# Edge stages of a graph layer: sums stored three slots to a transfer, and loads issued by ScalarE

## The reference

```
h = (x @ W.T).reshape(n, H, D)
alpha = einsum(h[src], a_src) + einsum(h[dst], a_dst)
enc = relu(edge_attr @ edge_W.T + edge_b).reshape(-1, H, D)
alpha = alpha + sum(enc * h[dst], axis=-1)
alpha = where(alpha >= 0, alpha, 0.2 * alpha)
ex = exp(alpha - segment_max(alpha, dst)[dst])
attn = ex / max(segment_sum(ex, dst)[dst], 1e-10)
out = segment_sum(h[src] * attn[..., None], dst) + bias
```

## Time and profile before

| | us |
|---|---|
| median of 3 runs | 7718.56 |
| lowest and highest run | 7714.73 and 7724.49 |
| span of the profiled execution | 7807.0 |
| PE busy | 5257.7 (67%) |
| POOL busy | 3613.4 (46%) |
| DVE busy | 3278.9 (42%) |
| ACT busy | 1371.0 (18%) |

### The profile page before, as it was taken

The page is one execution under the profiler, slowest core; times in us unless marked ns, Lnnn a source line. Parts: engine busy times, 40 slices in busy tenths (PEclk is TensorE's granted clock), DMA queues, the critical chain, the costliest instruction groups (busy, mean ns, idle before and its releaser), DMA issues. The chain is left out here.

```text
span 7807.0 us, 99204 instructions
## 1 busy us (share of the span) xinstructions
PE 5257.7 (67%) x19729; PEld 3739.4 (48%) x19729; DVE 3278.9 (42%) x5938; ACT 1371.0 (18%) x2977; POOL 3613.4 (46%) x3708
## 2 busy tenths in 40 slices
PE   2387887788788878228999625556565556663498
PEld 1144444444444444227999514444444444442498
DVE  6255555555555555721111313333333333336244
ACT  2122222222222222002222200000000000000122
POOL 2635555555555554042222056666666666650222
PEclk9689999999999999658999857777777777786699
DMA  6434444444444443515666544444444444434255
GB/s 220 136 101 122 122 119 123 124 124 125 122 123 121 122 124 102 186 60 165 183 183 183 153 102 114 113 115 115 114 112 113 113 114 116 113 102 154 101 198 188
DMA packets 718013, 1022.24 MB, mean 131 GB/s; under 512 B 301733, under 2 KB 531561, under 8 KB 692608
## 3 DMA queue, kind: packets, MB, share of 16 engines
q0 software_dynamic: 183456, 485.95, 23.8%
q1 hardware_dynamic: 527676, 519.31, 21.7%
q10 hardware_dynamic: 6564, 14.14, 0.5%
HBM read 868.26 MB, written 153.27 MB: 131 GB/s over the span
## 5 line engine op out<-in xcount | busy, mean ns | idle before, releaser
L773 POOL DMA_INDIRECT e_rows<-sc_table,e_eidx x3224 | 3115.9, 966 | 2253.8 <-issue 952.6
L880 PE MATMUL e_ps_o<-e_rows,e_oh 128*128 128x264 f32 x6448 | 1918.5, 449 | 856.9 <-ACT e_res L969 700.8
L880 PEld LDWEIGHTS e_ps_o<-e_rows,e_oh 128*128 128x128 f32 x6448 | 1379.2, 222 | 1384.3 <-issue 1147.6
L1064 DVE SCALAR_TENSOR_TENSOR e_u<-e_encr,e_adst,e_ps_hd 128x512 f32<-128x512 f32 x806 | 597.1, 745 | 1160.2 <-remote 366.1
L1132 DVE TENSOR_TENSOR e_rows<-e_rows,e_ps_w 128x1024 f32<-128x1024 f32 x806 | 970.7, 1207 | 106.3 <-issue 83.5
L822 PE MATMUL e_ps_X<-e_u,e_hwide 128*104 128x512 f32 x1612 | 871.1, 635 | 16.8 <-DVE e_u L1064 14.8
L1055 DVE TENSOR_SCALAR e_ohT<-e_at,e_nid 96x512 bf16<-96x512 int16 x806 | 292.5, 363 | 1384.6 <-DMA e_aw<-sc_a2p 553.7
L969 ACT COPY e_res<-e_ps_o 32x264 f32<-32x264 f32 x806 | 296.0, 367 | 3291.4 <-PE e_ps_o L884 1242.4
L810 PE MATMUL e_ps_enc<-e_at,e_w_enc 96*128 96x512 bf16 x806 | 317.9, 394 | 570.6 <-ACT e_encr L942 383.4
L1676 PE MATMUL x_ps_h<-x_xT,x_w 128*128 128x256 f32 x2624 | 648.2, 405 | 15.4 <-DMA x_b<-in_L_ffn_b_dram 15.4
L1676 PEld LDWEIGHTS x_ps_h<-x_xT,x_w 128*128 128x128 f32 x2624 | 638.5, 337 | 20.6 <-issue 16.4
(11 more groups left out here) (290 smaller groups left out, 3538.7 us busy)
## 6 DMA issues: line engine op xcount, KB each, us to landing
x_w<-in_L_ffn_W_dram SPq DMA_DIRECT2D x112, 1024.0 KB
e_at<-sc_grp SPq DMA_DIRECT2D x403, 192.0 KB
x_w<-in_L_ffn_w_dram SPq DMA_DIRECT2D x60, 1024.0 KB
e_rows<-sc_table,e_eidx POOLq DMA_INDIRECT x3224
e_at<-sc_grp SPq DMA_DIRECT2D x403, 96.0 KB
sc_agg<-e_res SPq DMA_DIRECT2D x816, 33.0 KB
sc_xb<-r_zero SPq DMA_DIRECT2D x24, 1032.0 KB
x_xin<-sc_xb SPq DMA_DIRECT2D x86, 258.0 KB
```

Of the source, the lines that this page charges most:

```text
L773: pool.indirect_dma_start(rows[:, k, s, j, :], None, dr["table"][:, :], bass.IndirectOffsetOnAxis(eidx[:, k, s, j:j + 1], 0)).then_inc(s_r ...
L880: nc.tensor.matmul(ps_o[:, 0:ROW], oh[:, k, at_j:at_j + P], rows[:, k, s, j, :], start=(j == 0), stop=False)
L1064: nc.vector.scalar_tensor_tensor(u[:, p, h, :], encr[:, h, :], adst[:, h:h + 1], ps_hd[:, h, :], ALU.add, ALU.mult).then_inc(s_u, 1)
```

## The change

The sums are no longer stored at their window's first node. `agg` gets 20512 rows instead of 6272 and 32, and slot number t stores at rows 32 t and on. Five groups of slots per block (3, 3, 3, 3 and 1) are stored by one transfer each, at an address that needs no table. Five semaphores, one per group, tell when a group is stored, and `evict` waits for one of them at slots 0, 3, 6, 9 and 12 only.

SP issues the loads of the first 4 slots (layer 0) or 2 slots (layer 1). All others are issued by ACT, in the new `ahead`, at the end of its work for a slot: a `hold` on PE, a TENSOR_LOAD of two registers, and the two DMAs, for the slot 4 or 2 places further on. In the prologue, `ahead` follows the relus of each slot of block 0 and of block 1 (in layer 1 it stands there alone).

The r-stage has to find a node's sums. In the last two blocks of layer 0, DVE works out for each of the 49 tiles of 128 nodes the row of `agg` that holds it (49 passes over 128x640 numbers and about a dozen small ones), and the result is kept for both layers. The r-stage then fetches the sums by 49 indirect DMAs of POOL, 7 per chunk, instead of 7 plain loads (L1304). The planning stage clears more rows of `agg` (9 transfers instead of 8) and writes two small tables less.

```
 SP
-            def store(t, s, n):
-                hold(sp, s_out, t * 16 - (32 * SB - OUT0), s_ps)
-                hold(sp, s_ev, t - (BEHIND - 1 - EV0), s_ps)
-                sp.dma_start(dr["agg"][bass.ds(n, WIN), :], res[0:WIN, kept((s - BEHIND) % SB), :]).then_inc(s_out, 16)
+            def store(b, g):
+                first_slot, end = GROUPS[g]
+                n, place = end - first_slot, kept(first_slot)
+                hold(sp, s_ev, b * SB + (EV0 + end), s_ps)
+                sp.dma_start(dr["agg"][bass.ds(b * (SB * WIN) + first_slot * WIN, n * WIN), :].rearrange("(s w) d -> w s d", w=WIN),
+                             res[0:WIN, place:place + n, :]).then_inc(s_out[g], 16)
...
             def phase(b, k):
-                for s in range(SB):
-                    t = b * SB + (2 * SB + s)
-                    hold(sp, s_hd if first else s_xa, t * PER - (behind(s) - 1) * PER, s_ps)
-                    g, n, back = entry(t)
-                    load(ring(s), g, n)
-                    store(t, s, back)
...
+                if not isinstance(b, int):
+                    store(b - 1, 3)
+                    store(b - 1, 4)
+                hold(sp, s_z, b + 1, s_ps)
+                flags((b + 2) * SB, k)
+                hold(sp, s_lk, b + 2, s_ps)
+                hold(sp, s_dn, b * 2 + 4, s_ps)
+                tables((b + 3) * SB, 1 - k)
+                for g in range(3):
+                    store(b, g)
 ACT
+            def ahead(b, s):
+                t, later = b * SB + (s + LEAD), (s + LEAD) % SB
+                if not isinstance(t, int) or t >= behind(later):
+                    hold(act, s_hd if first else s_xa, t * PER - (behind(later) - 1) * PER, s_pa)
+                load(act, t, ring(later))
...
-                if not isinstance(t, int) or t + BEHIND - 2 * SB + 1 >= since(s):
-                    hold(act, s_out, t * 16 + 16 * (BEHIND - 2 * SB + 2 - since(s)), s_pa)
+                if s in (6, 9):
+                    hold(act, s_out[s // 3 - 2], b * 16 + 16, s_pa)
+                elif s in (0, 3, 12) and not (isinstance(b, int) and b == 0):
+                    hold(act, s_out[{0: 2, 3: 3, 12: 4}[s]], b * 16, s_pa)
                 nc.scalar.copy(res[0:WIN, kept(s), :], ps_o[0:WIN, 0:ROW]).then_inc(s_ev, 1)
...
-            if first:
-                for s in range(SB):
+            for s in range(SB):
+                if first:
                     relu(0, s)
+                ahead(0, s)
             sources(0, 0, 0)
             leak(0)
             fade(0)
             power(0)
             place(0, 0)
-            if first:
-                for s in range(SB):
+            for s in range(SB):
+                if first:
                     relu(1, s)
+                ahead(1, s)
 DVE, layer 0
+                    if first and not pre:
+                        tile = (0 if turn else 2 * SB) + 2 * s
+                        if tile == 0:
+                            window_starts()
+                        for n in range(tile, min(tile + 2, NT)):
+                            slots_of(n)
 r-stage
-                    sp.dma_start(ag[:, c % 2, :, :], dr["agg"][c * R * P:(c + 1) * R * P, :].rearrange("(t p) d -> p t d", p=P)).then_inc(s_ag[c % 2], 16)
...
+                for c in range(R):
+                    if c >= 2:
+                        pool.wait_ge(s_agu, c - 1)
+                    for r in range(R):
+                        pool.indirect_dma_start(ag[:, c % 2, r, :], None, dr["agg"][:, :],
+                                                bass.IndirectOffsetOnAxis(nrow[:, c * R + r:c * R + r + 1], 0)).then_inc(s_ag[c % 2], 16)
```

More of the change, by code:

```diff
@@ L625, in edge_phase @@
             sem(n) for n in ("X", "y", "lk", "f", "b", "turn", "q", "f8", "mr", "mc", "al", "d", "col", "phi", "phb", "cf", "m"))
[L626 removed]
+        s_z, s_exp, s_wt, s_wc, s_sc, s_cs, s_o, s_ev, s_nst, s_code, s_row = (
+            sem(n) for n in ("z", "exp", "wt", "wc", "sc", "cs", "o", "ev", "nst", "code", "row"))
+        s_out = [sem(f"out{g}") for g in range(len(GROUPS))]
         s_pv, s_pp, s_pa, s_ps, s_pg = (sem(n) for n in ("pv", "pp", "pa", "ps", "pg"))
@@ L652, in steps_of, with entry, load @@
             return eng.value_load(nbi[0:1, 0:1], min_val=1, max_val=MAXSTEP)
+        LEAD = 4 if first else 2
+        def entry(eng, t):
+            why = "the planning stage writes only groups and starts of windows that lie inside their arrays"
+            _, vals = nc.values_load_multi_w_load_instructions(tab[0:1, bass.ds(t * 2, 2)], engines=[eng.engine], min_val=0, max_val=NP,
+                                                               skip_runtime_bounds_check_because=why)
+            return [nc.s_assert_within(x, 0, NG - 1 if c == 0 else NP, skip_runtime_bounds_check_because=why) for c, x in enumerate(vals)]
+        def load(eng, t, r):
+            g, n = entry(eng, t)
+            if first:
+                eng.dma_start(at[:, r, :, :].rearrange("q c e -> q (c e)"),
+                              dr["grp"][bass.ds(g, 1), :, :, :].rearrange("a m c e -> a m (c e)").to_broadcast([K3 // PARTS, PARTS, 2 * G])
+                              ).then_inc(s_ld[r], 16)
+                eng.dma_start(hp[:, r, :], dr["hp"][bass.ds(n, WIN), :, :].rearrange("n p d -> (n p) d")).then_inc(s_ld[r], 16)
+            else:
+                eng.dma_start(at[:, r, 1, :], dr["grp"][bass.ds(g, 1), 0, 1, :].to_broadcast([K3, G])).then_inc(s_ld[r], 16)
+                with nc.allow_non_contiguous_dma(reason="eight logits of a node's three parts"):
+                    eng.dma_start(aw[:, r, COLS - HEADS:COLS], dr["a2p"][bass.ds(n, WIN), :, :].rearrange("n p d -> (n p) d")).then_inc(s_ld[r], 16)
         block = ctx.enter_context(nc.Block())
@@ L664, in _ @@
                 sp.dma_start(w_st[3:4, :], io["L0_gnn_edge_b"].rearrange("(a o) -> a o", a=1)).then_inc(s_w, 16)
[L666 to L670, removed]
             def tables(t, k):
@@ L794, in _ @@
         def _(pe):
-            pe.wait_ge(s_const, 9 if first else 6)
+            pe.wait_ge(s_const, 10 if first else 6)
             pe.wait_ge(s_ready, 1)
@@ L1004, in _ @@
             phase(steps * 2 + 2, 0, False, False, 0)
+            for s in range(LEAD):
+                hold(act, s_ld[ring(s)], loads_of(steps * 2 + 3, s), s_pa)
         @block.vector
```

149 lines of the change are left out of this document (86 added, 63 removed).

## The result

The changed kernel takes 7874.06 us as the median of 4 runs (7866.18 to 7888.91), the kernel before 7720.24 us in the runs beside it. The ratio is 1.0204 with a 95% interval of 1.0192 to 1.0217. That is slower by 154 us, where +42 was forecast: the right sign, and less than a third of the size. In a later set on one chip the changed kernel, run once more, had a ratio of 1.0228 (1.0208 to 1.0249).

What follows compares the result with a forecast made beforehand. The prediction took PE's signals, arriving some 6 us late while POOL gathers, and not SP's loads or stores, to hold the edge stages. Its eight terms summed to +42 us, 7718.6 + 42 = 7760 us, range 7560 to 7920 us.

Steps and rivals of the forecast that it cites:

- 1 stores in layer 1: Layer 1: fewer and earlier stores shorten ACT's idle time before evicts; -45 us, ends 0 and -115.
- 2 ACT's work in layer 1: Layer 1: ACT's issue of loads fits into its idle time before evicts; +5 us, ends 0 and +30.
- 3 layer 0, steady: Layer 0 loop: ACT's 2.35 us issue delays evicts, 43 without slack; a third of 173 us, +60 us.
- 4 layer 0, prologue: Layer 0 prologue: 19 slots left behind the gathers take 1.65 us more each; +30 us, ends +10 and +55.
- 5 layer 1, prologue: Layer 1 prologue: softmax of block 0 starts 33 us earlier, block 1's loads follow it; -22 us, ends -40 and +10.
- 6 end of layer 0: Last two blocks of layer 0: DVE's 49 passes, a small store and a wait; +5 us, ends 0 and +33.
- 7 two r-stages: Both r-stages: gathers of 8.8 us hide behind DVE's 10.5 us chunks, only the first late; +6 us, ends 0 and +12.
- 8 planning: Planning stage: some 1 MB more to clear, beside DVE's work; +3 us, ends 0 and +8.
- Rival A: SP sets the pace of layer 1, so relieving it gains POOL's 442 us: 7585 us at half, 7364 in full; chance 0.22.
- Rival B: ACT gets as slow at issuing as SP while POOL gathers; at 5 us an issue +250 us in layer 0, 7950 us; chance 0.18.

Runs made afterwards that it cites:

- S: Kind of chip on which the kernel before took 7780 to 7793 us in the timed runs.
- F: Kind of chip on which the kernel before took 7712 to 7720 us in the timed runs.
- e2: e2_sp_loads: the changed kernel with the loads back on SP in both layers, sums still stored in groups; ratio to the kernel before 1.0023.
- e1: The kernel before, unchanged, profiled again on a chip of kind S; ratio 0.9999, span 7795.0 us.
- f2: f2_act_reads: e2 plus unused table reads on ACT, which the compiler removed, so e2 a second time, on kind F; ratio to the kernel before 1.0050.
- j0: The kernel before, run again on a chip of kind F; its profiled execution took 7740 us.
- j1: Layer 0 as in the kernel before; layer 1 with grouped stores, loads on SP, three r-stage buffers for its gathers; ratio to the kernel before 1.0045.
- e3: The changed kernel with ACT issuing the loads in layer 1 only, SP in layer 0; ratio to the kernel before 1.0041.
- e3b: The changed kernel with ACT issuing the loads in layer 0 only, SP in layer 1; ratio to the kernel before 1.0203.
- i4: The changed kernel, unchanged, run again on a chip of kind F; ratio to the kernel before 1.0228.
- i2_best: h2_act_nodes with three buffers instead of two for the sums gathered in the r-stage; ratio to the kernel before 1.0006.
- h3_act_groups: As e2, but in layer 0 ACT issues each slot's large load, three slots ahead, and SP the small one; ratio to the kernel before 1.0025.
- h2_act_nodes: As e2, but in layer 0 ACT issues each slot's small load, three slots ahead, and SP the large one; ratio to the kernel before 1.0006.
- f3_three_buffers: As e2, with three buffers instead of two for the sums gathered in the r-stage; ratio to the kernel before 1.0032.
- h0: The kernel before, run again on another chip; 6.91 us a slot in the steady part of layer 0.

## Why the prediction was wrong in size

Term by term, with what the runs showed:

| term | predicted | measured |
|---|---|---|
| 1 stores in layer 1 | -45 | -40 on S, -10 on F (e2 - e1, f2 - j0), -13 on F on one chip (j1 - j0) |
| 2 ACT's work in layer 1 | +5 | +12 in the 29 blocks (e3 - e2, 2298.0 and 2286.3); +16 by their medians, 7828.4 and 7812.2 |
| 3 layer 0, steady | +60 | +98 on S (e3b - e2), +102 on F on one chip (i4 - i2_best, 2687.2 and 2585.0), and +7 to +9 that is in e2 and f2 already |
| 4 layer 0, prologue | +30 | +20 (e3b - e1), +21 (i4 - j0) |
| 5 layer 1, prologue | -22 | +2 (e3 - e1, 170.8 and 169.1), 0 (i4 - j0) |
| 6 end of layer 0 | +5 | +9 (e2 - e1) |
| 7 two r-stages | +6 | +31 (e2 - e1) |
| 8 planning | +3 | +2 |

On F, i4 - f2 would give only +63 for term 3. That pair is from two chips, with one execution 20 us over its kernel's median and the other 23 under. The table gives some 100 to 130 us more than the +42. Term 3 has nearly 50 of them, and terms 1 (on F), 5 and 7 some 20 to 35 each.

**Term 3 is the step that failed most.** I worked out 173 us of later evicts and took a third, because PE "only waits where ACT's relu is behind". I counted waiting and nothing else. PE's idle time grew even less than my 60 us (0.06 us a slot or 21 us in the changed kernel against i2_best). What I put at nothing is that the matmuls themselves take longer: at a clock of 0.91 instead of 0.94, PE needs 0.25 us more for the same slot, 93 us. So the waits were priced too high and the clock not at all, and that the sum of the two came within a factor of two of the 60 is luck. The row that should have warned me was in the table: PE is busy for 1517.8 of 1900 us, so 3% of its speed is worth 45 us in that stretch and 63 us over the 29 blocks, as much as the whole term. The 43 evicts without slack, which made most of my 173 us, aren't enough by themselves: h3_act_groups puts 1.9 us ahead of each evict too, and its 29 blocks are 5 us longer than those of h2_act_nodes. That the slot took 7.15 us, as forecast, says little. On one chip it grew by 0.30 us, and not by the 0.19 between the two traces.

**Term 7 was wrong in its mechanism.** I compared seven gathers (8.8 us) with DVE's chunk (10.5 us) and found them hidden. With two buffers, POOL can't begin a chunk until DVE has freed one, 8.1 us into a chunk; the gathers took 11.0 us and their landing 4.7 us on top, 24 us for two chunks. f3_three_buffers took the loss away again, 10 to 11 us in each layer. The remaining 4 to 5 us in each lie ahead of the first chunk, the +3 that I had.

**Term 5 failed** at its first step. I let the softmax of block 0 begin as soon as block 0 was gathered, as if the loads ahead of it were quick on ACT. They weren't: ACT needed 9 to 13 us for each while POOL gathered, as SP had the earlier trace rows, and its softmax stands behind them:

```profile
4700.24 0.70 ACTq L668 DMA_DIRECT2D e_at<-sc_grp  x1
4705.13 1.40 ACTq L670 DMA_DIRECT2D e_aw<-sc_a2p  x1
4712.84 0.00 ACTq L668 DMA_DIRECT2D e_at<-sc_grp  x1
...
4726.20 0.54 ACT L957 COPY e_alog<-e_rows 128x416 f32<-128x416 f32 x1 [132.14 <-issue]
...
4758.67 0.51 ACT L973 COPY e_rows<-e_ps_w 128x416 f32<-128x416 f32 x1 [7.78 <-remote]
```

The softmax ended 12.3 us behind POOL's last gather (at 4746.3), and 1.5 us behind it before the change (4627.14 and 4625.6). The loads of block 1 then followed 1.6 us apart, twice as fast as assumed, and made that up. POOL idled 39.67 us in front of its next gather, 40.36 us before.

**What held.** Rival A, SP as the pace of layer 1, fell at the sizes that I gave it: SP is free for 920 us of 1900 and layer 1 keeps its late signals. A small part of it may be true. In the same stretch SP of the kernel before waited 6, 12 and 31 us on S (before, e1, h0), where grouping gained most, and 77 us on F (j0), where it gained least; no run tests this. Terms 4, 6 and 8 came out within 10 us of their values, and term 1 only on the slower kind of chip, from whose trace it was read. (In term 8 the rows to clear grow by 1.4 MB and not by 1, which made no difference.) Rival B, a slow ACT, is true for the prologue of layer 1, where its single instructions took up to 1.4 us, and not for the loop of layer 0, where register instructions of ACT took 0.04 us. Its middle price, +250 us in layer 0, was too high.

**The sum.** The changed kernel's ratio splits into 0.2 to 0.5% for everything but ACT's loads (e2_sp_loads, f2_act_reads), 1.8% for ACT's loads in layer 0, and about 0.2% for those in layer 1. At 7720 us these are some 27, 137 and 14 us, 178 together, just over the measured 154 to 176. The first and second share are from different chips, and the first alone varies by 0.3% between them.

**What stays open.** Why the issue of one load is free and copies of less time are not; whether the lower clock comes from longer pauses of PE; how much of the loss is the wait behind the relu (25 to 33 us with intervals that overlap); and why grouped stores bring 40 us in layer 1 on one chip and 10 on another.

## What to carry to other kernels

Work put into the queue of an engine that is 18% busy is not free if that engine answers the busiest one twice per step; look at the gap in which it must fit, and where PE is busy for 80% of a stretch, put a price on a lower granted clock as well as on the waits. An engine that never waits is not shown to be the limit by that; ask whether the others start when it finishes something. Compare stages of two traces only when runs beside them show the same time for the same kernel.

## What the runs showed of the hardware

- A signal from PE to ACT and POOL can arrive 6 us late while POOL's gathers flow, and this stayed with SP idle for half of the time and with the loads issued by ACT ("remote" 858.0 us).
- Issuing the same 192 KB load took 1.19 us from ACT as its median in the loop (L663), 0.77 us from SP.
- Instructions that only issue or count took up to 1.4 us on ACT and 2.1 us on SP in the prologue of layer 1 while POOL gathered, each where it issued the loads (SP before, ACT after).
- TensorE's granted clock, as a mean over the program, was 0.834 to 0.838 in the changed kernel, 0.839 to 0.844 with copies on ACT in place of the loads, and 0.844 to 0.851 in the kernel before.
- One kernel differs by 1% between chips (7712 and 7793 us) at the same mean granted clock (0.847), and an edit can gain 40 us in a stage on one and 10 us on another.
